# A six-layer local-attention kernel: Wv and Wo joined per head, exponentials per head on ScalarE, masks on VectorE, shifts by transfers

## The chip, the cores and the metric

The kernel runs on one core of one Trainium2 chip, in float32 throughout. Its time is the device time of one execution in microseconds (us), the median of several runs. Below, PE is TensorE, ACT is ScalarE, DVE is VectorE, POOL is GpSimd and SP is the queue that issues the transfers.

## What is computed

The input x is 4 sequences of 512 tokens with 128 numbers each. First comes one attention block with relative positions (16 heads of 8, all 512 keys), added to x. Then x is normalised and goes through six layers of local attention and gated feed-forward. The part around the change:

```python
for i in range(DEPTH):                                   # 6
    x = attn_layer(shift_tokens(x), Wqkv[i], ..., Wo[i]) + x
    x = ffn_layer(shift_tokens(x), ...) + x
# attn_layer
q, k, v = split(x @ Wqkv)                                # 16 heads of 64
q = l2norm(q) * qs;  k = l2norm(k) * ksc                 # then rotary, with a scale
sim = where(mask, -max, q @ k^T * 8.0)                   # windows of 32 queries, 64 keys
out = softmax(sim) @ v
return out @ Wo                                          # Wo: 1024 x 128
```

`shift_tokens` takes the second half of the 128 numbers from the token before. The norm of q is a positive factor per row and head, so it can be applied to the scores instead of to q. Since `softmax(sim) @ (x Wv) @ Wo` is linear in x, Wv and Wo of a head can be multiplied first (128 x 128 per head) and the probabilities can be applied to x itself.

## The kernel before

The program has two blocks. `relative_attention` (from L817) does the first attention in 128 rounds. Scores of positions go out to a scratch array in HBM and are read back shifted. At its end the next block, `local_layers` (from L45), projects the attention of all four sequences (`turn_attended` and `project_attended`, L583 to L593, and `add_attended`, `first_norm` in DVE's queue, L738 to L756), after x was loaded a second time.

`local_layers` works on tiles of 128 tokens. One layer has 16 tiles, four per sequence (a "group"), and the six layers have 96 tiles. The work of every engine is one queue in program order, written out by hand as a loop over periods `n`: in each period an engine handles one step of several tiles at different depths of the pipeline (from L606 for PE, and likewise for the others). An engine waits on semaphores where a step needs another engine's result. In period n, PE projects K, V and Q (L463), turns q and k by transposes (`turn_qk`, L473), makes masked scores: a bf16 product lays the mask into PSUM (L491) and 64 small products per tile add q k (L499). It transposes the probabilities (`turn_p`, L510), applies them to v in 64 products of 64 rows (`attend`, L529) and multiplies by Wo (`project_out`, L541). Once per group come the feed-forward steps: the shift by two products with a shifted identity (L551, L553), transposes (L561), `hidden` (L569) and `project_ffn` (L579).

PSUM has three pairs of banks (`ring`) and two single ones. `take` (L437) makes PE wait until the tile that last held the place has been read; `ROOM` and `FREED` (L118 to L122) say who shares a place with whom and who frees it.

ACT squares q and k out of PSUM (L317), takes the exponential of all 16 heads in one instruction (L363), copies xT, q, k, v, the probabilities and the output out of PSUM (L328 to L376), normalises (L393, eight instructions of 128x64 with scale and bias from memory) and does the gelus (L402). DVE makes the rotary products (L643), sums the squares (L652), takes maximum and difference of the scores (L658, L666), sums and divides the probabilities (L674, L687). POOL adds the rotary halves (L240), finds the norms by 14 small instructions (L248 to L265) and scales q and k by them (L275). SP places v into windows with 16 transfers per tile (`windows`).

## Time and profile before

| what | value |
|---|---|
| median of 3 runs (lowest, highest) | 2131.49 us (2127.36, 2133.46) |
| the profiled execution, own time | 2129.15 us |
| its span in the profile | 2127.4 us |
| busy: PE, DVE, ACT, POOL | 95%, 70%, 60%, 71% of the span |
| granted PE clock, mean | 0.987 of full speed |
| transfers | 261.5 MB, 41.3% of 16 engines' time on the main queue |

A profile lists for each engine when it was busy, and for each idle stretch what ended it. A busy PE is not a PE at its peak, since the ends of products are modelled. Groups of instructions are told by line; "mean ns" is the duration of one instruction, and two neighbours on an engine may overlap a little, so the distance between starts can be shorter than the duration. Float32 products appear as two instructions each. "PEclk" or the clock column is the clock granted to PE as a share of 2.4 GHz.

### The profile page before, as it was taken

The page shows a single profiled execution, that of the slowest core. Times are in us where ns is not written, and L with a number is a line of the kernel's source. Part 1 is how long each engine was busy: PE and PEld are TensorE (multiplying, and loading weights), DVE is VectorE, ACT ScalarE, POOL GpSimd, SP SyncE. Part 2 cuts the span into 40 slices and gives each one's busy share as a digit, 9 for nine tenths or more (in the row PEclk, how much of TensorE's full clock was granted, in tenths as well). Part 3 has the DMA queues.
Part 4 walks back from the last instruction along what each step waited for, and adds up shares of the span by engine and source line. Part 5 has one row for each costly group of instructions (what it writes and reads, how often), then busy time and mean ns, then how long its engine had stood idle before and what let it go on. Part 6 is the DMA issues. An engine that isn't in the chain of part 4 may idle for free.

```text
span 2127.4 us, 84221 instructions
## 1 busy us (share of the span) xinstructions
PE 2025.2 (95%) x35763; PEld 1357.7 (64%) x35763; DVE 1498.2 (70%) x2267; ACT 1285.3 (60%) x1844; POOL 1521.0 (71%) x2315
## 2 busy tenths in 40 slices
PE   6899998979999999999999999999999999999997
PEld 2555555545666667766676666766676666766665
DVE  3445454458877788778777788777787788777873
ACT  4676767535655666566655566566665666566653
POOL 4344444468888788777887788778887788877880
PEclk9999999989999999999999999999999999999998
DMA  6999999922224222242232322224222242222221
GB/s 201 331 347 354 340 352 351 328 73 59 65 67 115 63 66 70 62 114 62 63 73 63 111 68 66 63 64 112 67 72 64 61 118 62 67 63 63 66 70 41
DMA packets 121588, 261.51 MB, mean 123 GB/s; under 512 B 29140, under 2 KB 36224, under 8 KB 120448
## 3 DMA queue, kind: packets, MB, share of 16 engines
q1 hardware_dynamic: 121216, 256.13, 41.3%
q8 instruction: 285, 4.67, 0.9%
q14 instruction: 87, 0.71, 0.1%
HBM read 87.06 MB, written 68.29 MB: 73 GB/s over the span
## 4 chain that ended last, share of the span: by engine, by line
PE 72%; POOL 2%; DVE 2%; issue 1%; ACT 1%; POOLq 0%; DVEq 0%; ACTq 0%
PE ring L463 24%; PE ring L529 9%; PE ring L473 8%; PE yps L541 8%; PE ring L499 7%; PE ring L569 5%; PE ring L510 4%; PE tpose L579 3%; PE ring L491 1%; DVE turned L643 1%; PE tpose L551 1%; PE tpose L561 1%; POOL ropes L229 0%; POOL roped L275 0%; PE yps L454 0%
## 5 line engine op out<-in xcount | busy, mean ns | idle before, releaser
L643 DVE TENSOR_TENSOR turned<-ring,ropes 128x1024 f32<-128x1024 f32 x384 | 452.2, 1220 | 301.4 <-PE ring L463 301.4
L240 POOL TENSOR_TENSOR roped<-turned 128x512 f32<-128x512 f32 x384 | 522.1, 1385 | 171.8 <-PE ring L473 171.0
L463 PE MATMUL ring<-wqkv,xT 128*128 128x512 f32 x1152 | 565.2, 614 | 6.1 <-ACT xT L328 4.9
L275 POOL TENSOR_TENSOR roped<-roped,rnorm 128x1024 f32<-128x1024 f32 x192 | 361.2, 1902 | 7.5
L1188 POOL TENSOR_SCALAR less<-less,lowest 128x512 f32<-128x512 f32 x256 | 174.4, 692 | 216.1 <-DVE lowest L1141 216.1
L1141 DVE CUSTOM_DVE_ANT_0 less<-ps_b,shifted 128x512 f32<-128x512 f32 x256 | 166.7, 689 | 211.7 <-issue 89.5
L463 PEld LDWEIGHTS ring<-wqkv,xT 128*128 128x128 f32 x1152 | 197.6, 191 | 161.0 <-issue 149.3
L369 ACT COPY pT<-ring 128x1024 f32<-128x1024 f32 x96 | 97.1, 1012 | 305.3 <-PE ring L510 305.3
L529 PEld LDWEIGHTS ring<-pT,vwin 64*64 64x64 f32 x12288 | 198.3, 134 | 51.4 <-issue 51.1
L317 ACT ACTIVATE squares<-ring 128x1024 f32<-128x1024 f32 x192 | 197.2, 1027 | 55.0 <-DVE turned L643 54.9
L529 PE MATMUL ring<-pT,vwin 64*64 64x32 f32 x12288 | 219.4, 220 | 4.3 <-issue 2.6
L652 DVE TENSOR_REDUCE ss<-squares 128x16 f32<-128x1024 f32 x192 | 221.3, 1184 | 1.1 <-ACT squares L317 0.9
L473 PEld LDWEIGHTS ring<-ident,roped 128*128 128x128 f32 x1536 | 175.1, 142 | 72.1 <-issue 40.8
L473 PE MATMUL ring<-ident,roped 128*128 128x128 f32 x1536 | 205.4, 277 | 10.7 <-POOL roped L275 5.1
L499 PEld LDWEIGHTS ring<-kT,qT 64*32 64x32 f32 x12288 | 140.6, 105 | 98.3 <-issue 96.2
L541 PE MATMUL yps<-wo,oT 128*128 128x128 f32 x1536 | 187.4, 275 | 1.2 <-ACT oT L376 1.1
L972 PE MATMUL ps_b<-posm,qvT 32*128 32x512 f32 x512 | 147.1, 662 | 41.4 <-DVE lowest L1141 39.0
L541 PEld LDWEIGHTS yps<-wo,oT 128*128 128x128 f32 x1536 | 179.1, 192 | 1.6 <-ACT oT L376 1.6
L499 PE MATMUL ring<-kT,qT 64*32 64x64 f32 x12288 | 174.4, 224 | 2.3 <-issue 2.2
L1048 PEld LDWEIGHTS ps_b<-ident,less 128*128 128x128 f32 x1024 | 111.4, 142 | 93.6 <-POOL less L1188 76.9
L344 ACT COPY kT<-ring 128x1024 f32<-128x1024 f32 x96 | 97.0, 1011 | 101.7 <-PE ring L473 101.7
L1241 ACT ACTIVATE pT_a<-ps_b 128x512 f32<-128x512 f32 x256 | 141.5, 614 | 24.8 <-PE ps_b L1048 24.6
(134 smaller groups left out, 3242.0 us busy)
## 6 DMA issues: line engine op xcount, KB each, us to landing
vwin<-v SPq DMA_DIRECT2D x1536, 64.0 KB, 2.0
shifted<-scratch_w SPq DMA_DIRECT2D x64, 1024.0 KB, 12.0
scratch_w<-wrows SPq DMA_DIRECT2D x48, 1026.0 KB, 10.2
scratch_w<-x SPq DMA_DIRECT2D x16, 1026.0 KB, 9.9
wqkv<-in_l_wqkv SPq DMA_DIRECT2D x6, 1536.0 KB, 6.7
wo<-in_l_wo SPq DMA_DIRECT2D x6, 512.0 KB
w<-in_l_w SPq DMA_DIRECT2D x6, 342.0 KB
w<-in_l_w SPq DMA_DIRECT2D x6, 171.0 KB
```

Of the source, the lines that this page charges most:

```text
L240: nc.gpsimd.tensor_tensor(halves[2][:, :, side, :], halves[0][:, :, side, :], halves[1][:, :, 1 - side, :], ALU.add).then_inc(s[name + "_a ...
L275: nc.gpsimd.tensor_tensor(whole, whole, norm, ALU.mult).then_inc(s[name + "_roped"], 1)
L317: nc.scalar.activation(squares[:, n, :], ring[:, room(name.upper()), :, :].rearrange("p b c -> p (b c)"), ACT.Square).then_inc(s[name + "_ ...
L463: last = nc.tensor.matmul(out[:, half, :], xT[:, t % SEQT * P:(t % SEQT + 1) * P], wqkv[:, layer_of(t), at + half * 512:at + (half + 1) * ...
L473: last = nc.tensor.transpose(out[:, j * P:(j + 1) * P], roped[:, n, j * P:(j + 1) * P], ident[:, :])
L499: last = nc.tensor.matmul(out[W * win:W * win + W, r, j * W2:(j + 1) * W2], qT[rows, j, W * win:W * win + W], kT[rows, j, at:at + W2], sta ...
L529: last = nc.tensor.matmul(out[a * DH:(a + 1) * DH, r, at:at + W], vwin[rows, p, win, j * DH:(j + 1) * DH], pT[rows, j, W * win:W * win + W ...
L541: last = nc.tensor.matmul(out[:, 0:D], oT[:, j % 2, j // 2, :], wo[:, layer_of(t), j, :], start=j == 0, stop=j == PAIRS - 1)
L643: ins = nc.vector.tensor_tensor(turned[:, n, part, :].rearrange("p (h d) -> p h d", d=DH), heads, table, ALU.mult)
L652: nc.vector.tensor_reduce(ss[:, n * HEADS:(n + 1) * HEADS], squares[:, n, :].rearrange("p (h d) -> p h d", d=DH), AX.X, ALU.add).then_inc( ...
L1141: nc.vector.tensor_tensor_reduce(less[:, c % 2, k, :], ps[:, 2 + k, :], shifted[:, c // 2 % NR, k, c % 2, :], -SCALE0, HIGHEST, ALU.add, A ...
L1188: nc.gpsimd.tensor_scalar(less[:, c % 2, k, :], less[:, c % 2, k, :], -1.0, lowest[:, c % 2, k:k + 1], ALU.mult, ALU.add).then_inc(s["scal ...
```

## The change

- **V is not projected.** Once per layer PE transposes Wv (`turn_wv`, eight transposes) and multiplies it with Wo per head (`make_wvo`, 16 products), and ACT copies the results (`copy_wv`, `copy_wvo`). `attend` applies the probabilities to x itself, which `windows` has placed in windows by seven transfers per group: eight products of 32 rows, 128 columns of weights and 512 moving columns, in two sets of four that use the four row groups and four different banks. `project_out` has 16 products in place of eight.
- **The exponentials** are 16 instructions of 128x64 per tile, one per head, with the norm of q as scale and minus norm times maximum as bias, both from memory, and each gives its row sum (`accum_out`). POOL no longer scales q; DVE no longer sums the probabilities. `divide` moves from DVE to POOL, and the norms are found for two tiles at once.
- **The mask** is added by DVE as it takes the scores out of PSUM; the maximum is then taken from SBUF. The bf16 products and their tables go.
- **The probabilities are turned** by DVE (one transpose of 128x1024 in 32x32 blocks) in place of eight PE transposes and an ACT copy.
- **The shift** of the feed-forward is two transfers per group in place of two products.
- **The first attention** is finished per sequence: those of sequences 0 to 2 are projected, added and normalised within the attention block (`FINISH`), and only the last one in the second block. x stays in its buffer, the second load of it goes, and layer 0's Wqkv is loaded during the attention.
- **The orders** of all queues and the sharing of PSUM are new, and the pipeline is deeper: a tile's output is made five periods after its K, its group's feed-forward ends ten periods after the group's last K.

The new sharing of PSUM, as a line of the new kernel:

```python
ROOM = {"AT": 3, "AP": 4, "XT": 3, "K": 2, "Q": 0, "QT": 1, "KT": 1, "S": 0, "O0": 1, "O1": 2, "Y": 4, "XN": 3, "H0": 0, "H1": 1, "H2": 2, "F": 3, "WV": 1, "M0": 1, "M1": 1}
```

The core of the diff:

```diff
+            def windows(g):
...
+                at_least(sp, s["o_made"], SEQT * (g - 1))
...
+                         (xwin[0:up, p, 1:SEQT, 0, high], tiles[P - up:P, 0:SEQT - 1, high])]
+                for dst, src in moves:
...
+            def shift(g):
...
+                    tiles = x[:, g % BATCH * SEQT:(g % BATCH + 1) * SEQT, D // 2:D]
...
+                    sp.dma_start(xs[1:P, :, :], tiles[0:P - 1, :, :]).then_inc(s["shifted"], 16)
+                    sp.dma_start(xs[0:1, 1:SEQT, :], tiles[P - 1:P, 0:SEQT - 1, :]).then_inc(s["shifted"], 16)
...
+            def divide(t):
+                if live(t):
+                    pool.wait_ge(s["rinv_made"], t + 1)
+                    whole = probs[:, t % 2, :, :, :].rearrange("p r j k -> p (r j) k")
+                    nc.gpsimd.tensor_tensor(whole, whole, rinv[:, :, :].rearrange("p r j -> p (r j)").unsqueeze(2).broadcast_to(
+                        [P, HEADS, W2]), ALU.mult).then_inc(s["p_normed"], 1)
...
             for n in PERIODS:
-                step, g = n % SEQT, n // SEQT
+                add_b2(group_of(n - 13))
+                add(1, n - 1)
+                divide(n - 4)
                 norms(n - 2)
-                scale(0, n - 2)
-                scale(1, n - 2)
-                if step == 1:
-                    add_b2(g - 2)
+                scale_k(n - 2)
                 add(0, n - 1)
-                add(1, n - 1)
-                if step == 0:
-                    deviations(g - 2)
+                deviations(group_of(n - 9))
...
             def exps(t):
-                if live(t):
-                    act.wait_ge(s["scores_taken"], t + 1)
-                    flat = probs[:, t % 2, :, :, :].rearrange("p j r k -> p (j r k)")
-                    nc.scalar.activation(flat, flat, ACT.Exp, scale=QK_SCALE).then_inc(s["exped"], 1)
...
+                    at_least(act, s["p_normed"], t)
+                    for r in range(2):
+                        for j in range(PAIRS):
+                            h = 2 * j + r
+                            of_head = probs[:, t % 2, r, j, :]
+                            ins = nc.scalar.activation(of_head, of_head, ACT.Exp, scale=norm_of(t)[:, h:h + 1],
+                                                       bias=ebias[:, t % 2, r, j:j + 1],
+                                                       accum_out=rsum[:, r, j:j + 1])
+                    ins.then_inc(s["exped"], 1)
...
+            def copy_o(t, half):
+                if live(t):
+                    act.wait_ge(s["o_made"], t + 1)
+                    at_least(act, s["y_made"], t - 1)
+                    nc.scalar.copy(xpT[:, t % 2, :, 2 * half:2 * half + 2, :].rearrange("p h w q -> p w h q"),
+                                   pair("O" + str(half)).rearrange("p w (h q) -> p w h q", q=W)
+                                   ).then_inc(s["o_copied" + str(half)], 1)
...
             for n in PERIODS:
-                step, g = n % SEQT, n // SEQT
-                if step == 0:
-                    normalise(g - 2)
-                copy_p(n - 3)
-                if step == 0:
-                    copy_xn(g - 2)
+                copy_xn(group_of(n - 11))
+                copy_q(n - 2)
+                copy_next_wvo(n - 2)
+                gelus(group_of(n - 12), 2)
+                gelus(group_of(n - 12), 1)
+                gelus(group_of(n - 12), 0)
+                exps(n - 3)
+                square(1, n)
+                copy_k(n - 2)
+                copy_x(n + 1)
                 square(0, n)
-                exps(n - 2)
-                copy_q(n - 1)
-                square(1, n)
-                if step == 0:
-                    gelus(g - 2, 0)
-                    gelus(g - 2, 1)
-                    gelus(g - 2, 2)
-                copy_k(n - 1)
-                copy_o(n - 3)
-                copy_x(n + 2)
-                copy_v(n)
+                copy_o(n - 4, 0)
+                copy_o(n - 4, 1)
+                normalise(group_of(n - 9))
...
+            def attend(t):
+                if live(t):
+                    p = t // SEQT % 2
+                    pe.wait_ge(s["p_turned"], t + 1)
+                    pe.wait_ge(windows_in[p], WINDOWS * (t // SEQT // 2 + 1))
+                    take("O0", t)
+                    take("O1", t)
+                    for half in (1, 0):
+                        for win in range(WT):
+                            rows = slice(W * win, W * win + W)
+                            last = nc.tensor.matmul(pair("O" + str(win // 2))[:, win % 2, :], xwin[rows, p, t % SEQT, half, :],
+                                                    pT[rows, t % 2, :, half, :], start=half == 1, stop=half == 0)
+                    last.then_inc(s["o_made"], 1)
...
+            def project_out(t):
+                if live(t):
+                    for half in range(2):
+                        pe.wait_ge(s["o_copied" + str(half)], t + 1)
+                        pe.wait_ge(s["wvo_copied" + str(half)], t // (SEQT * BATCH) + 1)
...
+                    for h in range(HEADS):
+                        last = nc.tensor.matmul(out[:, 0:D], xpT[:, t % 2, h, :, :].rearrange("p w q -> p (w q)"),
+                                                wvo[:, layer_of(t), h // PAIRS, h % PAIRS, :], start=h == 0,
+                                                stop=h == HEADS - 1)
+                    last.then_inc(s["y_made"], 1)
...
+                    for j in range(PAIRS // 2):
+                        for r in range(2):
+                            rows, at = slice(r * DH, (r + 1) * DH), a * PAIRS // 2 + j
+                            last = nc.tensor.matmul(out[:, r, j * D:(j + 1) * D], wvT[rows, at, :], wo[layer % 2][rows, at, :],
...
             for n in PERIODS:
-                step, g = n % SEQT, n // SEQT
+                hidden(group_of(n - 12), 0)
+                turn_x(n + 1)
                 project("K", n)
+                project("Q", n)
+                turn_qk(1, n - 2)
+                project_out(n - 5)
+                attend(n - 4)
+                scores(n - 2, 0)
+                scores(n - 2, 1)
+                project_ffn(group_of(n - 13))
+                turn_xn(group_of(n - 10))
                 turn_qk(0, n - 1)
-                turn_x(n + 2)
-                if step == 0:
-                    hidden(g - 2, 0)
-                    hidden(g - 2, 1)
-                    hidden(g - 2, 2)
-                attend(n - 3, 0)
-                if step == 3:
-                    shift(g - 1)
-                if step == 1:
-                    project_ffn(g - 2)
-                turn_qk(1, n - 1)
-                attend(n - 3, 1)
-                project("V", n)
-                scores(n - 1, 0)
-                project("Q", n + 1)
-                scores(n - 1, 1)
-                turn_p(n - 2)
-                if step == 3:
-                    turn_xn(g - 1)
-                project_out(n - 3)
+                next_wvo(n - 1)
+                hidden(group_of(n - 11), 2)
+                hidden(group_of(n - 11), 1)
...
+                if live(t):
...
+                    dve.wait_ge(kept["made"], TABLES)
...
+                    nc.vector.scalar_tensor_tensor(probs[:, t % 2, :, :, :].rearrange("p r j k -> p (r j) k"),
+                                                   pair("S").rearrange("p r (j k) -> p (r j) k", k=W2), QK_SCALE, seen,
+                                                   ALU.mult, ALU.add).then_inc(s["scores_taken"], 1)
...
+            def exp_bias(t):
...
+                    dve.wait_ge(s["rnorm_made"], t // 2 + 1)
+                    at_least(dve, s["exped"], t - 1)
+                    norm = norm_of(t)[:, 0:HEADS].rearrange("p (j r) -> p r j", r=2)
+                    nc.vector.scalar_tensor_tensor(ebias[:, t % 2, :, :], smax[:, :, :], -1.0, norm, ALU.mult, ALU.mult
+                                                   ).then_inc(s["ebias_made"], 1)
...
+            def turn_p(t):
+                if live(t):
+                    dve.wait_ge(s["p_normed"], t + 1)
+                    at_least(dve, s["o_made"], t - 1)
+                    nc.vector.transpose(pT[:, t % 2, :, :, :].rearrange("p h s q -> p (h s q)"),
+                                        probs[:, t % 2, :, :, :].rearrange("p r j k -> p (r j k)")).then_inc(s["p_turned"], 1)
...
             for n in PERIODS:
-                step, g = n % SEQT, n // SEQT
-                if step == 2:
-                    add_ffn(g - 2)
+                sum_squares(1, n - 1)
+                sum_squares(0, n - 1)
+                offsets(group_of(n - 10))
+                add_y(n - 6)
+                take_scores(n - 3)
+                take_max(n - 3)
+                exp_bias(n - 3)
+                gate(group_of(n - 12), 1)
+                add_ffn(group_of(n - 14))
+                gate(group_of(n - 12), 2)
+                statistics(group_of(n - 9))
+                turn_p(n - 4)
+                gate(group_of(n - 12), 0)
+                rotate(1, n)
                 rotate(0, n)
-                take_max(n - 2)
-                take_scores(n - 2)
-                add_y(n - 4)
-                rotate(1, n)
-                if step == 3:
-                    statistics(g - 1)
-                sum_probs(n - 2)
-                invert(n - 2)
-                sum_squares(0, n)
-                if step == 0:
-                    gate(g - 2, 0)
-                    gate(g - 2, 1)
-                    gate(g - 2, 2)
-                sum_squares(1, n)
-                if step == 3:
-                    offsets(g - 1)
-                divide(n - 2)
-                if 1 <= n < BATCH:
-                    first_norm(n)
+                invert(n - 3)
+                if n == 8:
+                    first_norm()
             dve.wait_ge(s["x_done"], GROUPS)
...
+            FINISH = {85: 0, 93: 1, 101: 2}
...
-                    sp.wait_ge(written[0], in_slot(written, ROUNDS // 2 - NW))
-                    sp.dma_start(x1, x_in).then_inc(kept["x1_loaded"], 16)
-                    sp.wait_ge(kept["x1_loaded"], 16)
+                    sp.wait_ge(s["c_taken"], 2 * 2 * ROUNDS // BATCH)
+                    sp.dma_start(kept["early"][:, 0:3 * INNER], layers["wqkv"][0]).then_inc(kept["qkv0_loaded"], 16)
...
```

## Rows read from the trace of the kernel before

**Rows 1.** Windows: us, then busy (instructions) of PE PEld DVE ACT POOL, clock, DMA share, GB/s.
```profile
105.00:435.00 330.00, 299.00 (x3520) 180.88 (x3512) 159.52 (x497) 224.48 (x433) 148.63 (x219) 1.00 0.98 335
442.00:505.00 63.00, 48.28 (x490) 29.95 (x490) 46.58 (x79) 25.11 (x33) 47.54 (x76) 0.81 0.27 79
505.00:2040.00 1535.00, 1526.06 (x29733) 1053.02 (x29733) 1206.72 (x1469) 936.08 (x1216) 1240.64 (x1894) 1.00 0.29 74
```

**Rows 2.** One line of the feed-forward shift matmul, made once in four tiles: first and last start.
```profile
L551 PE MATMUL tpose<-x,down x48: 379/431/483, 562.0 to 2102.4; 128*128 128x256 f32 x48
```

**Rows 3.** Chain of waits across one tile of the layers: start, us, engine, line.
```profile
1017.03 1.02 PE ring L510 x8
1018.06 1.79 PE yps L541 x16
...
1022.55 1.06 PE ring L529 x64
...
1025.76 1.91 PE ring L463 x4
1027.67 0.34 PE ring L491 x8
...
1030.71 0.79 PE ring L499 x53
1031.50 1.03 PE ring L510 x8
```

**Rows 4.** Timeline of PE, feed-forward of one group: start, us, line, tile.
```profile
1006.17 2.94 PE L579 MATMUL tpose<-w,hT 114*128 114x128 f32 x24
...
1052.76 5.31 PE L569 MATMUL ring<-xnT,w 128*114 128x512 f32 x12
```

**Rows 5.** Timeline of PE in the attention stage, around one round of scores.
```profile
201.80 0.69 PE L972 MATMUL ps_b<-posm,qvT 32*128 32x512 f32 x1
...
202.87 1.09 PE L1048 MATMUL ps_b<-ident,less 128*128 128x128 f32 x8
```

**Rows 6.** Groups of ScalarE by form, 900 to 1300 us: busy us, mean ns, idle before.
```profile
L317 ACT ACTIVATE squares<-ring 128x1024 f32<-128x1024 f32 x47 | 48.3, 1027 | 10.6 <-DVE turned L643 10.6
L363 ACT ACTIVATE probs<-probs 128x1024 f32<-128x1024 f32 x24 | 25.4, 1059 | 13.9 <-DVE probs L666 13.9
...
L344 ACT COPY kT<-ring 128x1024 f32<-128x1024 f32 x24 | 24.3, 1011 | 26.8 <-PE ring L473 26.8
...
L402 ACT ACTIVATE gelu<-ring,b 114x512 f32<-114x512 f32 x18 | 11.7, 685 | 2.0 <-PE ring L569 2.0
L393 ACT ACTIVATE xn<-x,offset,rstd 128x64 f32<-128x64 f32 x24 | 10.4, 434 | 2.7 <-DVE offset L713 2.7
...
L402 ACT ACT_TABLE_LOAD x6 | 7.7, 1283 | 0.1
```

**Rows 7.** Timeline of ScalarE around one normalise.
```profile
1041.96 0.26 ACT L328 COPY xT<-yps 64x128 f32<-64x128 f32 x1
...
1044.41 0.44 ACT L393 ACTIVATE xn<-x,offset,rstd 128x64 f32<-128x64 f32 x1 [0.46 <-DVE offset L713]
...
1046.61 0.40 ACT L393 ACTIVATE xn<-tpose,offset,rstd 128x64 f32<-128x64 f32 x1
```

**Rows 8.** Chain of waits: a joint from ScalarE to TensorE.
```profile
474.12 0.14 issue
```

**Rows 9.** Groups of VectorE by form, 900 to 1300 us.
```profile
L643 DVE TENSOR_TENSOR turned<-ring,ropes 128x1024 f32<-128x1024 f32 x94 | 110.7, 1220 | 76.3 <-PE ring L463 76.3
...
L666 DVE TENSOR_TENSOR probs<-ring,smax 128x1024 f32<-128x1024 f32 x23 | 28.2, 1224 | 0.8
```

**Rows 10.** Groups of GpSimd by form, 900 to 1300 us.
```profile
L275 POOL TENSOR_TENSOR roped<-roped,rnorm 128x1024 f32<-128x1024 f32 x47 | 88.5, 1902 | 1.8
```

**Rows 11.** Timeline of PE, first matmuls of the layers.
```profile
442.05 1.09 PE L585 MATMUL ring<-ident,x 128*128 128x128 f32 x8 [1.74 <-PEq L913]
```

**Rows 12.** DMA issues of the page: KB each, us to landing.
```profile
wqkv<-in_l_wqkv SPq DMA_DIRECT2D x6, 1536.0 KB, 6.7
```

624 lines of the change are left out of this document (319 added, 305 removed).

## The prediction

> **What bounds the kernel now.** I read the windows first. In the steady part of the layers PE is busy 1526 of 1535 us, while DVE has 79% of it, POOL 81% and ACT 61%, all at the full clock [rows 1]. So PE sets the pace there, and the others wait for it. The product that shifts tokens runs once in four tiles and starts from 562.0 to 2102.4 us, in 24 groups [rows 2]: 1540.4 / 92 = **16.74 us per tile**, or 1607 us for the 96. The layers' block begins at 442.05 [rows 11]. What is left of the span is 2127.4 - 442 - 1607 = 78 us, for filling and draining the pipeline. The profiled execution took 2129.15 us, 1.75 more than its span and 2.3 less than the median of the runs.
>
> The chain of waits shows a tile without feed-forward as a solid row of PE work, from 1017.03 to 1031.50, or 14.47 us [rows 3]. Feed-forward and shift bring the mean to 16.74.
>
> **What PE does after the change, per tile.** From 14.47 go V (1.91), the mask products (0.34) and the turning of the probabilities (1.02) [rows 3]. Eight more products in `project_out` add as much as the eight there now, 1.79 [rows 3]. `attend` becomes eight products of 32 rows by 512. Four of this shape, in four row groups, take 202.87 - 201.80 = 1.07 us in the attention stage [rows 5], so two sets take 2.14, as the two halves of 1.06 do now [rows 3]. The plain tile is then 13.0 us. The group's feed-forward is 5.31 + 2.94 [rows 4] and half of a 1.02 us turn, 8.8 us or 2.2 per tile. The joined weights cost one turn of 1.02 and 16 products at the rate of `project_out` (3.6), 4.6 per layer or 0.3 per tile. PE's sum is **15.5 us**, 1.25 less than now. If PE stayed the bound, that alone would be 96 x 1.25 = 120 us less.
>
> **What ACT does after the change.** The exponential of a tile is one instruction of 1.06 now. It becomes 16 of 128x64 with scale and bias from memory. The nearest are those of `normalise`, of the same shape and with the same kinds of operands: 0.434 us each from SBUF [rows 6]. Eight of them run from 1044.41 to 1047.01 [rows 7], 0.325 from start to start, since neighbours overlap by 0.1. No row has an instruction of ACT that also gives a sum. Its price lies between nothing (0.325 a head, 5.2 a tile) and a further small instruction behind each, like the smallest there is, 0.26 [rows 7] (0.70 a head, 11.2 a tile). I take it that the sum must be complete before the next head starts, so that the overlap is lost: 0.434 a head, **6.9 us a tile**. That is the nearest row at its full duration. Squares and copies of q, k and two of the output at 0.9 from start to start, with 0.5 for xT, add 6.0, and the group's part (three gelus of 0.69, two table loads of 1.28, eight of 0.325 and a copy) 8.0 or 2.0 per tile [rows 6, 7]. ACT's sum is 15.1, level with PE's 15.5, so the order of the queues decides.
>
> **The loop through the queues.** In ACT's new order `exps(n-3)` stands ahead of `square(1, n)` and `copy_k(n-2)`. PE's `attend(n-4)` puts its output where kT (ring 1) and K (ring 2) were, so it waits for both. `scores(n-2)` stands behind `attend(n-4)` on PE. DVE then takes scores, maximum and bias, and only then can ACT begin the next tile's `exps`. Round that loop once per tile:
> - exponentials 6.9; square and copy, 1.03 + 1.01 less 0.1 of overlap, 1.94 [rows 6]
> - joint to PE 0.14 [rows 8]; `attend` 2.14; scores twice 0.79, 1.58 [rows 3, 5]
> - two passes of DVE over 1024 numbers, 1.22 each [rows 9], and the small bias, 0.2 with its joints (my estimate)
>
> That is 8.5 + 6.9 = 15.4 us for a plain tile, where PE needs 13.0. `copy_o` and `copy_q` fit in while ACT waits. What stands between the scores and the next exponentials in some tiles comes on top of it, since DVE's path there is only 2.6 long. In the gelu tile PE turns q (1.02) and does `hidden` (5.31), then a gelu (0.69) and a table load (1.28) follow: 8.3, or 5.6 more. In the tile of `project_ffn`, 2.94, the turn and `copy_q` make 5.0, 2.3 more. `normalise` makes 1.0 more. That is 8.9 per four tiles, 2.2 per tile, and the three steps of the joined weights some 1.5 each in 16 tiles, 0.3. **The tile takes 15.4 + 2.2 + 0.3 = 17.9 us.** In short it is the exponentials plus 11.0.
>
> **What lies beside it.** DVE turns the probabilities in place of summing and dividing them. No row shows that transpose: between one pass of 1.22 [rows 9] and three of them it stays covered, since DVE has 6.9 us under the exponentials for it and the 2.4 of k's rotary products. The mask with the scores is again a pass out of PSUM, 1.22. `divide` on POOL costs what the scaling of q does there now, 1.90 [rows 10], a change of place; with half of the norms gone POOL's sum falls below its present 13.5 (81% of 16.74). If the exponentials took less than the turn and k's rotary products on DVE, 1.2 + 2.4 us, DVE would set the loop in their place. SP issues nine transfers per group in place of 64. The shifted halves land while DVE takes the next scores, so I cost them at nothing; uncovered they would be 2 us per group, 48 in all.
>
> **Ends.** The attention stage is bound by transfers: DMA is busy 98% at 335 GB/s, PE 91%, DVE 48% [rows 1]. Layer 0's 1.5 MB [rows 12] then cost up to 4.6 us there. Finishing three sequences lies under the transfers. I take +5, with 0 and +15 as ends. The second block turns and projects one sequence in place of four (-7) and makes layer 0's joined weights (+5). Its last tile drains later by 10 (long exponentials, shift by transfer, longer `project_out`), and the first three tiles run without exponentials (-18): 78 - 10 = 68, of which I keep 63, since the clock of 0.81 at the start [rows 1] falls on less work.
>
> **Sum.** 442 + 5 + 96 x 17.9 + 63 = 2228, and 1.75 outside the span: **2230 us**, 4.7% more than the profiled execution.
>
> **The rivals.**
> - **The sums are free and the kernel is faster.** At 0.325 a head the exponentials take 5.2 and the tile 16.2. The total is 2230 - 96 x 1.7 = 2067, near PE's own bound (15.5 per tile gives 2000). It decides below the point where 96 tiles fit in 2129 - 2 - 510 = 1617 us, 16.84 a tile: exponentials of 5.8, or 0.365 a head. For it: the overlap in `normalise` is real. Against it: nothing there is summed. The Trainium skill, page "ScalarE: Activation LUTs", section "What ACT_TABLE_LOAD costs", has 186 ns plus 0.833 per element plus 93 per pointer operand, 425 here, and an overlap of 93 between neighbours; the trace agrees. It prices no accumulator output, so read alone it gives 0.332 a head and this rival's time.
> - **The sum is an instruction of its own** that costs 0.14 to 0.26 beyond 0.434. The middle of 9.1 us per tile gives 20.1 a tile and 2440; the far end of 11.2 gives 2640.
> - **The clock falls.** With PE waiting for ACT its busy share drops to 15.5 / 17.9 = 87%. It ran at 1.00 with 91% in the attention stage and at 0.81 with 77% in the start of the layers [rows 1]. If `attend` and the scores (3.7) ran at 1.2 GHz in half of the tiles, that is 1.9 more per tile, 2410. The skill's "TensorE: Matmul & The Clock Gate", "What's actually happening", says that the throttled state is the default and activity releases it, which speaks against any change that makes PE wait.
> - **`attend` does not do what it says**, and its four row groups run one behind the other: eight at half of V's 1.91 are 7.6, 5.5 more, 2760. Against it: [rows 5] show the same shape side by side.
>
> **Chances.** The forecast has 0.48 and its own range is 2140 to 2340. The free sums have 0.27, the separate instruction 0.15, the clock 0.06, the serial `attend` 0.04. The range from 2050 to 2420 takes in the first two and the lower half of the third. A measurement of this kernel tells 0.3%, some 6 us, from no change. Faster is the free-sum rival, 0.27; between, where 0.36 to 0.37 a head would fall, 0.03; slower 0.70.
>
> **What would show it.** Right: the `exps` line of ACT at 16 x 96 instructions with about 0.43 from start to start; PE idle before `attend` and before scores, released by ACT's copy of kT; ACT idle before `exps`, released by DVE's bias; PE busy near 87% and 71.6 us between groups of four tiles. Wrong: no idle PE, a tile near 15.5 to 16.2, or heads 0.33 apart. A step would fail alone if DVE's transpose took over 4 us, if `attend` took over 2.2, or if the stage before 450 us grew by more than 15.

## The result, and the profile after

The kernel takes **2368.32 us** (median of 4 runs, 2367.31 to 2369.5) against 2132.47 for the kernel before: a ratio of 1.1107, 95% interval 1.108 to 1.1133. The forecast was 2230, in a range of 2050 to 2420. The direction and the range hold, but the kernel lost 236 us where I forecast 98. The profiled execution took 2367.31 us, 1.8 more than its span.

The page of the changed kernel, its span, busy times, chain by engine and by line, and two of its costliest groups (busy us, mean ns of one, idle time before):

```profile
span 2365.5 us, 63006 instructions
...
PE 1913.9 (81%) x24771; PEld 1279.3 (54%) x24771; DVE 1435.8 (61%) x2267; ACT 1752.9 (74%) x4740; POOL 1304.7 (55%) x1639
...
ACT 29%; PE 25%; issue 9%; DMA 8%; DVE 8%; SPq 1%; POOL 0%; ACTq 0%; DVEq 0%; POOLq 0%
...
L395 ACT ACTIVATE probs<-probs,ebias,rnorm 128x64 f32<-128x64 f32 x1536 | 652.8, 427 | 42.2 <-DVE ebias L717 41.7
...
L395 ACT ACTIVATION_READ_ACCUMULATOR probs<-probs,ebias,rnorm 128x1 f32 x1536 | 288.5, 188 | 0.0
```

PE has less to do than before (1913.9 us busy, 2025.2 then), and still the span grew by 238. No engine fills it: the kernel went from bound by an engine to bound by a loop through several. The windows, with the columns of [rows 1], say it by stage:

```profile
105.00:435.00 330.00, 295.54 (x3485) 180.62 (x3482) 164.49 (x521) 225.81 (x432) 152.97 (x223) 1.00 1.01 341
...
560.00:2040.00 1480.00, 1208.78 (x16536) 835.50 (x16538) 982.86 (x1256) 1180.11 (x3390) 892.57 (x1072) 0.94 0.08 19
```

The attention stage runs on its transfers as before (DMA share 1.01, and 0.98 then). In the layers PE went from 99% busy [rows 1] to 82%, its granted clock from 1.00 to 0.94 in the mean, and DMA from 0.29 to 0.08: the transfers that the change removed were never what was waited for. The wait that took the place of a busy PE is the forecast one, at `attend` for kT (PE's longest wait by line: us in all, times, longest):

```profile
PE ring L558 <- ACT kT L383: 274.8, 93, 7.8
```

**The loop.** This is one plain tile in the chain of waits (start, us, what):

```profile
1030.04 0.91 ACT squares L357
1030.94 0.91 ACT kT L383
...
1032.09 2.00 PE ring L558 x16
1034.09 1.43 PE ring L541 x91
...
1035.54 1.24 DVE probs L699
...
1036.80 1.23 DVE smax L706
...
1038.06 0.37 DVE ebias L717
...
1038.45 4.39 ACT probs L395 x21
...
1047.40 2.00 PE ring L558 x16
```

It is the loop of the prediction, member by member: square and copy, joint, `attend`, scores, two passes of DVE, bias, exponentials, and `attend` again. Round it took 47.40 - 32.09 = **15.31 us, forecast 15.4**. So the miss isn't there, though the agreement is in part luck: the exponentials, `attend` and the scores took 0.1 each less than forecast, the bias with its joints 0.3 more. The starts of `attend` through the whole seventh group of four tiles show where it is (PE's timeline of that line; the brackets are the idle time before it):

```profile
1032.09 2.00 PE L558 MATMUL ring<-pT,xwin 32*128 32x512 f32 x16 [1.76 <-ACT kT L383]
1047.40 2.00 PE L558 MATMUL ring<-pT,xwin 32*128 32x512 f32 x16 [2.11 <-ACT kT L383]
1068.07 2.00 PE L558 MATMUL ring<-pT,xwin 32*128 32x512 f32 x16 [2.21 <-ACT kT L383]
1087.19 3.45 PE L558 MATMUL ring<-pT,xwin 32*128 32x512 f32 x16 [5.02 <-ACT kT L383]
1105.70 2.00 PE L558 MATMUL ring<-pT,xwin 32*128 32x512 f32 x16 [1.77 <-ACT kT L383]
```

The plain tile takes 15.31, the gelu tile 20.67 (forecast 15.4 + 5.6), the tile with the shift and `normalise` 19.12 (forecast 15.4 + 1.0), the tile of `project_ffn` 18.51 (forecast 15.4 + 2.3). The shift's tile is 2.7 us too long. In it the chain leaves the loop:

```profile
1068.29 1.03 ACT squares L357
...
1070.48 0.29 DVE x L738
...
1070.79 0.70 SPq L224
...
1071.54 8.49 DMA xs<-x
...
1080.06 0.05 DVE stats L745
...
1082.66 2.33 DVE turned L680 x2
...
1085.93 1.02 ACT kT L383
...
1087.19 3.45 PE ring L558 x16
```

**The transfer of the shifted halves takes 8.49 us**, and the statistics wait for it on DVE with k's rotary products queued behind them; kT is late by that, and `attend` with it. The rows of the shift buffer, all 24 groups (min/median/max in ns, then DVE's idle time and number of times):

```profile
L224 SPq DMA_DIRECT2D xs<-x x24: 692/700/703, 609.2 to 2332.5; - x24
L225 SPq DMA_DIRECT2D xs<-x x24: 6427/6499/6546, 609.9 to 2333.3; - x24
...
  DVE stats L745: 113.6, 24
```

I had costed this at nothing. DVE waits 113.6 us for it in 24 groups, and the issue of the second, small transfer takes 6.5 us of SP. The `attend` after the wait then ran at the lower of TensorE's two clocks, 3.45 us for the same 16 products that take 2.00 (window with the columns of [rows 1], granted clock 0.55):

```profile
1087.00:1090.50 3.50, 3.31 (x16) 1.30 (x16) 2.94 (x6) 1.37 (x3) 2.96 (x5) 0.55 0.00 0
```

It is not the only one. Of the 96 starts of `attend`, 43 took longer than the 2.00 us of the full clock, up to 3.80, and these durations add up to 63 us above 2.00. In the 21 groups of the table below, among them are 20 of the 21 with which the `project_ffn` tile starts, after waits of 2.7 to 7.0 us, and 11 of the 21 with which the gelu tile starts. There the wait was some 2.1 us in the slow cases and in most of the fast ones alike, so the wait just before doesn't settle which clock it gets.

**Smaller changes in the profile.** The transpose, unknown before, is one pass of DVE like the others; the small bias product is the group that surprises (groups of VectorE by form, 900 to 1300 us, columns of [rows 9]):

```profile
L731 DVE STREAM_TRANSPOSE pT<-probs 128x1024 f32<-128x1024 f32 x21 | 25.7, 1223 | 0.0
...
L717 DVE SCALAR_TENSOR_TENSOR ebias<-smax,rnorm 128x16 f32<-128x16 f32 x20 | 11.3, 564 | 0.7
```

It handles 16 numbers per partition and takes 0.56 us in the mean, where I had taken 0.2 with its joints.

### The profile page after: what moved, and what is told of

Its sections match the earlier page's. It is cut to its first block, busy times and chain, and to the rows that moved or that the text cites. A ratio compares the mean times of both kernels' runs of the same rounds, so it can differ in the third digit from the quotient of the medians.

```text
span 2365.5 us, 63006 instructions
## 1 busy us (share of the span) xinstructions
PE 1913.9 (81%) x24771; PEld 1279.3 (54%) x24771; DVE 1435.8 (61%) x2267; ACT 1752.9 (74%) x4740; POOL 1304.7 (55%) x1639
## 4 chain that ended last, share of the span: by engine, by line
ACT 29%; PE 25%; issue 9%; DMA 8%; DVE 8%; SPq 1%; POOL 0%; ACTq 0%; DVEq 0%; POOLq 0%
ACT probs L395 19%; PE ring L558 9%; DMA xs<-x 8%; PE ring L620 5%; PE ring L541 5%; ACT kT L383 4%; ACT squares L357 4%; PE tpose L631 3%; DVE turned L680 2%; PE ring L524 2%; DVE probs L699 1%; DVE smax L706 1%; ACT L395 1%; DVE stats L745 1%; SPq L224 1%
## 5 line engine op out<-in xcount | busy, mean ns | idle before, releaser
L395 ACT ACTIVATE probs<-probs,ebias,rnorm 128x64 f32<-128x64 f32 x1536 | 652.8, 427 | 42.2 <-DVE ebias L717 41.7
L558 PE MATMUL ring<-pT,xwin 32*128 32x512 f32 x1536 | 255.0, 789 | 280.2 <-ACT kT L383 274.8
L277 POOL TENSOR_TENSOR roped_k<-turned 128x512 f32<-128x512 f32 x192 | 239.9, 1271 | 227.7 <-PE ring L524 123.3
L570 PE MATMUL yps<-wvo,xpT 128*128 128x128 f32 x3072 | 358.8, 275 | 2.7 <-issue 2.7
L570 PEld LDWEIGHTS yps<-wvo,xpT 128*128 128x128 f32 x3072 | 350.7, 192 | 3.4 <-issue 3.4
L277 POOL TENSOR_TENSOR roped_q<-turned 128x512 f32<-128x512 f32 x192 | 239.7, 1270 | 155.1 <-PE ring L524 155.0
L405 ACT COPY xpT<-ring 128x1024 f32<-128x1024 f32 x192 | 185.1, 1015 | 148.9 <-PE ring L558 148.9
L395 ACT ACTIVATION_READ_ACCUMULATOR probs<-probs,ebias,rnorm 128x1 f32 x1536 | 288.5, 188 | 0.0
L319 POOL TENSOR_TENSOR probs<-probs,rinv 128x1024 f32<-128x1024 f32 x96 | 182.7, 1903 | 103.7 <-DVE rinv L724 103.5
L511 PE MATMUL ring<-wqkv,xT 128*128 128x512 f32 x384 | 175.2, 599 | 5.9 <-DVE gelu L763 5.9
```

Of the source, the lines that this page charges most:

```text
L277: nc.gpsimd.tensor_tensor(halves[2][:, :, side, :], halves[0][:, :, side, :], halves[1][:, :, 1 - side, :], ALU.add).then_inc(s[name + "_a ...
L319: nc.gpsimd.tensor_tensor(whole, whole, rinv[:, :, :].rearrange("p r j -> p (r j)").unsqueeze(2).broadcast_to([P, HEADS, W2]), ALU.mult).t ...
L395: ins = nc.scalar.activation(of_head, of_head, ACT.Exp, scale=norm_of(t)[:, h:h + 1], bias=ebias[:, t % 2, r, j:j + 1], accum_out=rsum[:, ...
L405: nc.scalar.copy(xpT[:, t % 2, :, 2 * half:2 * half + 2, :].rearrange("p h w q -> p w h q"), pair("O" + str(half)).rearrange("p w (h q) -> ...
L511: last = nc.tensor.matmul(out[:, half, :], xT[:, t % SEQT * P:(t % SEQT + 1) * P], wqkv[layer_of(t)][:, at + half * 512:at + (half + 1) * ...
L558: last = nc.tensor.matmul(pair("O" + str(win // 2))[:, win % 2, :], xwin[rows, p, t % SEQT, half, :], pT[rows, t % 2, :, half, :], start=h ...
```

## The experiments

Three suspects stood: the price of the sums, the shift transfer and, more weakly, the clock and the bias product. In the expectations, which were written before each run, theory A is the loop with the sums and the transfer as its costs; the other letters are explained where they stand. The kernel before took 2130.21, 2130.47 and 2128.39 us in the three sets of runs, and ratios are to it.

The tiles of the table are means over 21 whole groups, from the seventh `attend` of the profile to the 91st: the intervals from `attend` to `attend` of the plain, gelu, shift and `project_ffn` tiles. The seventh group, read above, is the shortest of the 21 in the changed kernel (73.61 us, mean 76.28), so single intervals of it can mislead. The last column is what all 96 `attend`s took above 2.00 us each, that is, at the lower clock.

| kernel | time, us | ratio, 95% | mean tiles, us | sum | `attend` above 2.00, us |
|---|---|---|---|---|---|
| changed kernel | 2368.32 | 1.108 to 1.1133 | 15.66, 22.16, 19.18, 19.28 | 76.3 | 63 |
| sums left out | 2256.8 | 1.0554 to 1.0611 | 14.15, 20.10, 19.19, 18.57 | 72.0 | 44 |
| shift left out | 2299.64 | 1.0759 to 1.0829 | 15.63, 21.87, 16.79, 19.34 | 73.6 | 53 |
| both left out | 2116.74 | 0.9917 to 0.9954 | 14.18, 20.37, 15.12, 17.01 | 66.7 | 13 |
| small transfer first | 2383.78 | 1.1151 to 1.122 | 15.76, 21.86, 19.80, 19.46 | 76.9 | 60 |
| shift by tile | 2299.13 | 1.0759 to 1.0815 | 15.61, 22.09, 16.53, 19.12 | 73.4 | 58 |
| shift in 112 + 15 partitions | 2298.52 | 1.0755 to 1.0826 | 15.70, 22.24, 16.40, 19.00 | 73.3 | 50 |
| bias from PSUM | 2355.31 | 1.1027 to 1.1087 | 15.55, 22.16, 19.18, 19.29 | 76.2 | 62 |
| PE kept busy | 2363.86 | 1.107 to 1.113 | 15.43, 21.52, 19.20, 19.97 | 76.1 | 35 |
| sums on VectorE | 2244.28 | 1.0508 to 1.0561 | 14.13, 20.14, 19.19, 18.08 | 71.5 | 43 |
| three mends together | 2117.42 | 0.9915 to 0.9959 | 14.13, 19.99, 14.93, 16.93 | 66.0 | 11 |
| four mends together | 2092.32 | 0.9797 to 0.984 | 13.76, 20.08, 14.36, 16.71 | 64.9 | 2 |

**1. The sums left out.** The row sums are a constant, so the output is not the reference's.

```diff
 nc.scalar.activation(of_head, of_head, ACT.Exp, scale=norm_of(t)[:, h:h + 1],
-                     bias=ebias[:, t % 2, r, j:j + 1],
-                     accum_out=rsum[:, r, j:j + 1])
+                     bias=ebias[:, t % 2, r, j:j + 1])
...
+nc.gpsimd.memset(rsum[:, :, :], 16.0).then_inc(s["ready"], 1)
```

> The 16 exponentials give no sums (the row sums are a constant 16 set once, so the probabilities are not normalised and the output is not the reference's); everything else is as after the change. Theory A (the tile is a loop through ACT's exponentials, kT's copy, attend, scores and DVE): without the read-out of the sum neighbours overlap again, about 0.33 us a head in place of 0.43, 1.6 us less per tile, and the plain tiles shorten by that until PE is the bound: 2210 to 2250 us in place of 2368. Rival B (the shift's transfer and the clock set the pace, the exponentials lie under something else): 2340 us or more. A also expects PE's idle time before attend to fall from about 2.7 to about 1 us per tile.

Measured 2256.8 us (2252.61 to 2257.79), 7 above the upper end. The seventh group's plain and gelu tile lose 1.48 us each, 16 x 0.0925: the heads are that much nearer. The shift's tile doesn't move at all (19.18 and 19.19 in the mean). The chain of this kernel in that tile says why:

```profile
1026.41 8.49 DMA xs<-x
...
1034.92 0.05 DVE stats L745
```

With shorter exponentials the transfer alone sets the tile. So the sums cost 111.5 us, and hide part of what the transfer costs.

**2. The shift left out.** The statistics wait for the sums of the residual instead, and the shifted half is zero, so this output isn't the reference's either.

```diff
-sp.dma_start(xs[1:P, :, :], tiles[0:P - 1, :, :]).then_inc(s["shifted"], 16)
-sp.dma_start(xs[0:1, 1:SEQT, :], tiles[P - 1:P, 0:SEQT - 1, :]).then_inc(s["shifted"], 16)
...
-dve.wait_ge(s["shifted"], 32 * (g + 1))
+dve.wait_ge(s["y_added"], SEQT * (g + 1))
```

> The two transfers of the shift are left out and the shifted half is zero (so the feed-forward sees a zero half and the output is not the reference's); DVE's statistics wait only for the output tiles. Theory A: DVE stood idle before the statistics for 113.6 us in 24 groups with the rotary products of k queued behind; it gets back most of that, 75 to 110 us: 2260 to 2290 us. Rival C (that wait lies beside ACT's loop and costs next to nothing, what is above the forecast comes from the clock): 2345 us or more, with as many half-clock stretches as before.

Measured 2299.64 us, 69 less than the changed kernel and 10 above the expected range. The shift's tile falls by 2.4, from 19.18 to 16.79 in the mean, and the others hardly move.

**3. Both left out**, the two edits in one kernel.

> Both together: no sums from the exponentials and no shift transfers (the probabilities are not normalised, the shifted half is zero). Theory A: the two add up until PE's own 15.5 us per tile bounds the loop, 16.0 to 16.4 us per tile, 2100 to 2150 us. If the two costs were the same wait seen twice, the time would be near the lower of the two single ones, above 2200.

Measured 2116.74 us (2111.99 to 2124.93 in 10 runs): 251.6 us less, where the parts alone give 111.5 + 68.7 = 180.2. The table has the reason. In the shift's tile the edits bring nothing and 2.4 alone, and 4.1 together: whichever of the two waits is taken out, the other stands behind it. In the next tile they bring 0.7, nothing and 2.3, and there 1.1 of it is the `attend` that starts it, 3.45 us in the mean of the changed kernel and 2.32 here. Over all `attend`s the time above 2.00 falls from 63 to 13 us, where the edits alone take off 19 and 10. So some 20 of the 71 us that the two bring beyond their sum are clock, and most of the rest is the shift's tile. The windows of this kernel, 900 to 1300 us:

```profile
900.00:1300.00 400.00, 362.81 (x4987) 254.46 (x4986) 297.04 (x386) 326.85 (x660) 273.82 (x330) 0.98 0.07 16
```

PE is back at 91% and the granted clock at 0.98, from 82% and 0.95. This kernel beats the kernel before by 0.6%, though with work left out. So what the change loses is these two costs and what they do together.

**4. The small transfer first.** Is the 8.5 us that of the second transfer, which is issued for 6.5?

```diff
+sp.dma_start(xs[0:1, 1:SEQT, :], tiles[P - 1:P, 0:SEQT - 1, :]).then_inc(s["shifted"], 16)
 sp.dma_start(xs[1:P, :, :], tiles[0:P - 1, :, :]).then_inc(s["shifted"], 16)
-sp.dma_start(xs[0:1, 1:SEQT, :], tiles[P - 1:P, 0:SEQT - 1, :]).then_inc(s["shifted"], 16)
```

> Only the order of the two shift transfers is exchanged: the small one (3 rows of 256 bytes, into partition 0) goes first, the large one (508 rows of 256 bytes) second. Theory D (the second issue takes 6.5 us because the queue still works off the 508 rows of the first, and the large one's rows themselves need those 6.5 us): no gain, within 10 us of 2368, the landing stays near 8.5 us after the issue. Theory E (the large one lands soon, about 2 us like the v transfers of before, and only the small one behind it is late): 60 to 90 us less.

Measured 2383.78 us, 15 more, where theory D had at most 10; theory E falls. SP's timeline and DVE's longest wait for a transfer (us in all, times, longest):

```profile
1069.63 0.72 SPq L224 DMA_DIRECT2D xs<-x  x1
1070.41 0.74 SPq L225 DMA_DIRECT2D xs<-x  x1
```

```profile
DVE stats L745 <- DMA xs<-x: 127.2, 24, 10.0
```

Both issues are now short, and the wait is longer. So the long issue was the small transfer standing behind the large one; the large one is slow by itself.

**5. The shift by tile**: seven transfers per group, each issued when its tile's residual is there.

```diff
-sp.wait_ge(s["y_added"], SEQT * (g + 1))
...
+for t in range(SEQT):
+    sp.wait_ge(s["y_added"], SEQT * g + t + 1)
+    sp.dma_start(xs[1:P, t:t + 1, :], tiles[0:P - 1, t:t + 1, :]).then_inc(s["shifted"], 16)
+    if t + 1 < SEQT:
+        sp.dma_start(xs[0:1, t + 1:t + 2, :], tiles[P - 1:P, t:t + 1, :]).then_inc(s["shifted"], 16)
```

> The shift's transfers go out tile by tile as each tile's output is added (four of 127 rows of 256 bytes and three of one row), so that only the last tile's transfer lies between the last add and the statistics. Theory D (a transfer takes by its number of 256-byte rows): the last landing comes some 3 us after the add in place of 8.6 and the two DVE passes cover it; the gain is near that of leaving the shift out: 2295 to 2320 us. Rival F (each transfer takes its 8 us whatever its rows, or seven issues cost the queue more than two): 2350 us or more.

Measured 2299.13 us (ratio 1.0759 to 1.0815), the time of the kernel without a shift. Only the last quarter is left to come after the last residual, and DVE waits for it once in 24 groups, for 3.4 us.

**6. The shift in 112 and 15 partitions.** Is it the 508 rows of 256 bytes, or the 127 partitions?

```diff
-sp.dma_start(xs[1:P, :, :], tiles[0:P - 1, :, :]).then_inc(s["shifted"], 16)
+for lo, hi in ((1, P - 15), (P - 15, P)):
+    sp.dma_start(xs[lo:hi, :, :], tiles[lo - 1:hi - 1, :, :]).then_inc(s["shifted"], 16)
```

> The same 508 rows of 256 bytes of the shift in two transfers, 112 partitions and 15, in place of one of 127. Theory H (127 partitions go to one DMA engine, which works off 508 rows alone; 112 spread over 16 and 15 over 15): the landing falls from 8.5 us after the issue to 2 to 4, and the gain is near that of leaving the shift out, 2290 to 2315 us in place of 2368. Rival D (the number of rows sets the time, however they are spread): within 15 us of 2368.

Measured 2298.52 us, as without a shift, with the same bytes in the same rows and one transfer more. SP's timeline of this kernel, and its statistics from 560 to 2260 us, by form:

```profile
1046.25 1.54 SPq L225 DMA_DIRECT2D xs<-x  x2
1047.84 0.73 SPq L226 DMA_DIRECT2D xs<-x  x1
```

```profile
L746 DVE BATCH_NORM_STATS2 stats<-x 128x6 f32<-128x64 f32 x92 | 19.1, 207 | 0.4 <-DMA xs<-x 0.4
```

DVE waits 0.4 us in that stretch, where the changed kernel waits 103.5 for the same line. The statistics of the seventh group start at 1050.58, 2.0 us after the last issue ends, when DVE has finished the bias product. How busy the DMA engines were while each kernel's shift was under way shows the difference, first the changed kernel and then this one (columns of [rows 1]; the last two are DMA share and GB/s):

```profile
1071.60:1080.00 8.40, 7.16 (x47) 5.10 (x47) 3.56 (x3) 4.59 (x17) 2.49 (x2) 1.00 0.08 18
```

```profile
1047.00:1048.60 1.60, 1.60 (x11) 1.30 (x12) 1.56 (x2) 1.11 (x2) 0.48 (x1) 1.00 0.38 79
1048.60:1050.50 1.90, 1.90 (x6) 0.76 (x5) 1.87 (x2) 0.42 (x1) 1.90 (x2) 1.00 0.01 2
```

The number of rows isn't the cost; the shape is. The Trainium skill, page "DMA: Bandwidth & Descriptors", section "🔬 Why a DMA increments its semaphore by 16 and not by 1", says that a transfer is spread over the largest number of engines up to 16 that divides its slowest dimension. By that, 127 partitions go to one engine, 112 to 16 and 15 to 15. The traces agree: a share of 0.08 for 8.4 us, where one engine of 16 would be 0.06, and 0.38 in the split kernel, whose engines are idle (0.01) 2.4 us after its first issue began.

The other tiles stay within 0.3 us of the changed kernel's in the mean.

**7. The bias product from PSUM.** The maxima go to a free corner of the scores' bank, so the product has one operand in SBUF and one in PSUM.

```diff
-nc.vector.tensor_reduce(smax[:, :, :].rearrange("p r j -> p (r j)"),
+nc.vector.tensor_reduce(ring[:, ROOM["S"], 0, 0:HEADS],
...
-nc.vector.scalar_tensor_tensor(ebias[:, t % 2, :, :], smax[:, :, :], -1.0, norm,
+nc.vector.scalar_tensor_tensor(ebias[:, t % 2, :, :], ring[:, ROOM["S"], 0, 0:HEADS].rearrange("p (r j) -> p r j", r=2), -1.0, norm,
...
-"S": ("scores_taken",),
+"S": ("ebias_made",),
```

> As after the change, but DVE writes the maxima into the scores' own PSUM bank, so that the small bias product has one input in SBUF and one in PSUM in place of two in SBUF; PE's next Q waits for that product in place of the scores' own pass. Theory L (the product of 16 columns, 0.56 us in the mean and up to 1.9, waits for the end of POOL's instruction under way because both of its inputs are in SBUF): its mean falls to about 0.2 us and the loop shortens by up to 0.35 us per tile: 2335 to 2355 us. Rival M (it waits for something else, the write of the norms for one): mean unchanged, 2360 us or more.

The product in the changed kernel, and then in this one (min/median/max in ns):

```profile
L717 DVE SCALAR_TENSOR_TENSOR ebias<-smax,rnorm x96: 174/354/1861, 503.8 to 2304.5; 128x16 f32<-128x16 f32 x96
```

```profile
L716 DVE SCALAR_TENSOR_TENSOR ebias<-ring,rnorm x96: 173/174/176, 500.5 to 2291.0; 128x16 f32<-128x16 f32 x96
```

The durations became one. With both operands in SBUF they depended on what GpSimd did. The changed kernel's timeline (start, us):

```profile
522.17 1.90 POOL L313 TENSOR_TENSOR roped_k<-roped_k,rnorm 128x1024 f32<-128x1024 f32 x1
522.66 1.45 DVE L717 SCALAR_TENSOR_TENSOR ebias<-smax,rnorm 128x16 f32<-128x16 f32 x1
```

The product ends within 0.04 us of POOL's instruction. The Trainium skill, page "GPSIMD Engine Reference", section "8. Key points", says that GpSimd shares its way to SBUF with VectorE, and that VectorE's instructions with two SBUF inputs contend with it; the pair of kernels agrees, with 1861 ns at worst against 176. The time fell only to 2355.31 us, by 13, at the upper end of what was expected: the plain tile lost 0.18 (median 15.32 to 15.14), as it should (354 - 174 ns). In the shift's tile the product had been long (1.12 us in the seventh group), but what it gave up there DVE waited for the transfer:

```profile
DVE stats L744 <- DMA xs<-x: 126.3, 24, 9.3
```

That is 12.7 us more than the 113.6 of the changed kernel. Beside the other mends, where the transfer is covered, the same edit was worth 25 us (experiment 10).

**8. PE kept busy.** If the clock is what costs, give PE something to do while it would wait: the first eight output products are done twice.

```diff
 out = take("Y", t)
+for h in range(PAIRS):
+    nc.tensor.matmul(out[:, 0:D], xpT[:, t % 2, h, :, :].rearrange("p w q -> p (w q)"),
+                     wvo[:, layer_of(t), h // PAIRS, h % PAIRS, :], start=h == 0, stop=h == PAIRS - 1)
 for h in range(HEADS):
```

> As after the change, but PE makes the first eight output products of a tile twice (1.8 us more PE work per tile, ahead of attend, where PE waits for ACT; the result is the same). Theory K (part of the loss is the half clock that PE gets after waiting: attend and scores then take 1.5 us longer): the granted clock rises above 0.937 and the time falls, 2325 to 2360 us. If the clock costs nothing: 2365 to 2375 us, the work lies in idle time. If PE's work is on the path after all: up to 2540 us (96 x 1.8 more).

Measured 2363.86 us, ratio 1.107 to 1.113: no gain that can be told from none. The time lies above what theory K expected and just below what no cost of the clock would give. PE's wait for kT at `attend` fell from 274.8 to 126.1 us and the mean clock rose from 0.937 to 0.955. The tiles show two effects that cancel. None of the gelu tile's 21 `attend`s is slow any more, where 11 were, and that tile is 0.6 us shorter in the mean. Before the `project_ffn` tile 18 of 21 stay slow, and the tile is 0.7 us longer. So, by the gelu tile, the clock does cost time on this loop; what a full clock throughout would be worth stays open.

**9. The sums on VectorE.** The same sums by a reduction of the exponentials. The exponentials no longer wait for the divide of the tile before, since they don't write the sums.

```diff
-at_least(act, s["p_normed"], t)
...
-                     bias=ebias[:, t % 2, r, j:j + 1],
-                     accum_out=rsum[:, r, j:j + 1])
+                     bias=ebias[:, t % 2, r, j:j + 1])
...
+nc.vector.tensor_reduce(rsum[:, :, :].rearrange("p r j -> p (r j)"),
+                        probs[:, t % 2, :, :, :].rearrange("p r j k -> p (r j) k"), AX.X, ALU.add
+                        ).then_inc(s["p_summed"], 1)
+dve.wait_ge(s["p_summed"], t + 1)
```

> ACT's exponentials give no sums; DVE sums the probabilities in one pass, as the kernel before did (1.2 us a tile), just before the reciprocal. Theory A: ACT's loop gets 1.6 us shorter and DVE, 61% busy, has room for the pass outside of it: 2255 to 2285 us, at most 25 us behind the run without any sums. Rival G (the pass stands ahead of the squares' sums of the next tile and delays the scores): 2330 us or more.

Measured 2244.28 us, 11 below the expected range and 12.5 less than without any sums. So 96 reductions cost nothing that can be seen: DVE had the room. Why it beats the kernel without them isn't settled. The only difference in its favour is the wait that it drops; the difference lies in the `project_ffn` tile (18.08 for 18.57 in the mean).

**10. The mends together.** Sums on VectorE, the shift by tile, and `project_ffn` issued after the turn of q, so that q isn't late in that tile:

```diff
-project_ffn(group_of(n - 13))
 turn_xn(group_of(n - 10))
 turn_qk(0, n - 1)
+project_ffn(group_of(n - 13))
```

> Sums on DVE, the shift tile by tile, and on PE the feed-forward projection moved behind the turn of q, so that ACT's copy of q does not wait for it. Theory A: both costs that made the change slow are gone without leaving work out; 15 to 30 us above the run without sums and shift, 2125 to 2150 us, so about level with the kernel before. If the DVE pass became the bound: 2200 or more.

Measured 2117.42 us (2108.08 to 2121.39), ratio 0.9915 to 0.9959, 8 below the expected range. Then with the bias product from PSUM too, once with the shift in 112 + 15 partitions and once by tile:

> The sums on DVE, the projection behind the turn of q, the shift in transfers of 112 and 15 partitions, and the maxima in PSUM. If H and L hold: 5 to 35 us below the version with the shift tile by tile (2117), 2080 to 2112 us, and PE near its own 15.5 us per tile. If PE already bounds that version: within 5 us of 2117.

> The version with the shift tile by tile, the sums on DVE and the projection behind the turn of q (2117 us), with the maxima in PSUM added alone. Theory L: the bias product falls from 0.49 to 0.2 us, and what is left of ACT's loop shortens: 2095 to 2113 us. If PE bounds that version: within 5 us of 2117.

Measured 2094.3 us (0.981 to 0.9855), as expected, and **2092.32 us** (0.9797 to 0.984), 3 below its range; the two don't differ. The windows of the last, 900 to 1300 us:

```profile
900.00:1300.00 400.00, 367.56 (x5149) 257.31 (x5147) 321.78 (x418) 334.56 (x671) 281.26 (x337) 1.00 0.08 19
```

PE is 92% busy at the full clock, and `attend` took longer than 2.00 us once in 96. This version does all of the work, with the sums back on VectorE, and is 1.8% faster than the kernel before, where the change as it was made is 11% slower.

## Why the prediction was right, and where it failed

- **The bound moves from PE to the loop through the queues**: right. The chain has its members in the forecast order, and the plain tile 15.31 us against 15.4.
- **Exponentials at 0.434 a head**: right in size. The heads of one tile start 0.43 apart and 16 take 6.9 us. The reason was half right, so the close number is partly luck. ScalarE's timeline (start, us) shows an instruction that I had only as a bound:

```profile
1038.45 0.44 ACT L395 ACTIVATE probs<-probs,ebias,rnorm 128x64 f32<-128x64 f32 x1 [0.44 <-DVE ebias L717]
1038.80 0.19 ACT L395 ACTIVATION_READ_ACCUMULATOR probs<-probs,ebias,rnorm 128x1 f32 x1
1038.89 0.43 ACT L395 ACTIVATE probs<-probs,ebias,rnorm 128x64 f32<-128x64 f32 x1
```

  A read-out of 188 ns follows each head, overlapping with both neighbours, and the head costs 0.43 where it costs 0.34 without (1.48 / 16 = 0.0925 less). The rival of the separate instruction named the mechanism, with a price of 0.14 to 0.26 beyond 0.434; the price beyond it is nothing. The rival of the free sums falls: at 13.84 a plain tile their absence is worth 111.5 us.
- **`attend` side by side**: right, 16 products in 2.00 us (forecast 2.14). The serial rival falls.
- **The transpose on DVE, and POOL's divide**: right, 1.22 us, within the bounds, and covered; the divide 1.90.
- **The shift transfers**: here the step failed. I wrote that "the shifted halves land while DVE takes the next scores, so I cost them at nothing", with 2 us per group as the uncovered end. The transfer takes 8.49 us, and what covers it, scores, maximum and bias on DVE, ends earlier: DVE idled 4.7 us per group (113.6 / 24). Nothing in the trace before had that shape, and I took no bound from a row for it. In place of 0 (or 48) the runs show 69 us (experiments 2, 5 and 6), and 140 once the sums are gone (2256.8 - 2116.74).
- **The bias at 0.2**: too small; it was an estimate without a row. The mean was 0.56. Its effect on the time is 13 us alone, 25 beside the mends. A small slip stands beside it: the terms of ACT's sum, 6.9 + 6.0 + 2.0, give 14.9 and not 15.1, and nothing hangs on it.
- **The clock**: a rival with 0.06 and a price of 180 us, partly true on top of the forecast. The mean is 0.937. 43 of 96 `attend`s took longer than 2.00 us, up to 3.80, 63 us in all; the scores behind the one of 3.45 took 1.48 us where they take 1.42. The single mends left most of it (35 to 62 us), and with both costs out or mended it is nearly gone (13 to 2 us). The 63 us are read from the trace. No run takes out the clock alone, so how much of them lies on the path isn't measured.
- **The tile as a sum.** From one start of the statistics to that of 22 groups later (618.63 to 2290.05) a tile takes 18.99 us, against 17.9. The table's stretch gives 76.3 a group, where the forecast has 71.6. Tile by tile, without the joined weights, the excess is 0.3 in the plain tile, 1.2 in the gelu, 2.8 in the shift's and 1.6 in the `project_ffn` tile. The slow `attend`s account for 0.1, 0.8, 0.1 and 1.4 of these. So the shift's tile is the transfer, and the gelu and the `project_ffn` tile are longer mostly by what their slow `attend`s are. The joined weights were right: the five groups that make them take 79.1 in the mean, the other sixteen 75.4, which is 0.23 per tile for a forecast of 0.3. In all the tiles make 1.09 x 96 = 105 us of the miss.
- **The ends.** The layers begin at 453.35, 11.3 later for a forecast of 5; DMA is as full there as before. The remainder is 2365.5 - 453.35 - 96 x 18.99 = 89 us, for 63. The drain from the last tile's `attend` took 48.1 us (2317.38 to the end) for 30.9 before (2096.48 to the end), so 17 more where I had 10. The rest of the 26 must lie in the start, where the first tiles saved less than I took. Together with the 6 us above that is 32 us. None of it was tried alone.

The sum closes: the forecast span of 2228, and 105 + 6 + 26, give 2365 us. Of the 138 us of miss, 69 are the transfer by experiment; up to 63 are the clock, as read from the trace; and 32 are the ends, which weren't tried. The three overlap in part, since they add up to more than the miss.

## What to carry to other kernels

A transfer between two places on the chip is a step with a duration, even if it replaces 64 others: look for what covers it, for how long, and check that its partition count divides well; 127 partitions cost 8.5 us where 112 and 15 were covered. When an engine-bound kernel becomes loop-bound, single mends are worth less than their duration, since the next wait takes part of the gain: the bias product gave 13 us alone and 25 once the transfer was covered. The clock came back only when the waits were gone together. Try mends together before giving one up. A small instruction on the loop counts in full: of the 1.65 us between plain tiles of 15.31 and 13.66, 1.48 are 16 read-outs of a sum and 0.18 is one product of 16 columns.

## What the runs showed of the hardware

- An activation that also sums is two instructions, the second 188 ns long; the pair costs 0.09 us more per head than the activation without it.
- A transfer of 127 partitions x 4 x 256 bytes within SBUF took 8.49 us; the next transfer's issue on the same queue stood for 6.5. It kept the DMA engines 0.08 busy. In 112 + 15 partitions all three issues took 2.3 us, and the DMA engines, 0.38 busy, were idle from 2.4 us after the start of the first.
- A product of VectorE with both inputs in SBUF, 128x16, took from 174 to 1861 ns beside GpSimd's work; with one input in PSUM always 173 to 176.
- In the layers TensorE's mean granted clock was 1.00 with PE 99% busy (kernel before) and 0.94 with 82% (changed kernel), where 16 products of 32x512 took 2.00 us or up to 3.8.
- DVE's transpose of 128x1024 float32 in blocks of 32x32 took 1.22 us, as long as its other passes over 1024 numbers.
